# Attention over 8192 context rows on one core: turned keys made two stages early, written to device memory and read back

## What is computed

```
q = xn @ Wq                      # 128 x 1024 per batch
k, v = split(ctx @ Wkv)          # 2048 x 1024 each per batch
q = l2norm(q) * q_scale;  k = l2norm(k) * k_scale      # per head of 64
sim = einsum('bhid,bhjd->bhij', q, k) * 8
out = softmax(sim) @ v           # with the null key and value in front
return layer_norm((out, heads joined) @ Wout, g_out)
```

## Time and profile before

| | us |
|---|---|
| median of 3 runs | 1401.02 (1400.99 to 1401.05) |
| the profiled execution's own time | 1405.52 |
| its span | 1403.7 |
| PE busy in it | 1220.3 (87%) |
| DVE, ACT, POOL busy | 641.4, 439.2, 314.4 |
| the long block's loop, first query product to last output | 787.66 to 1320.96 |

### The profile page before, as it was taken

How to read it: one execution, slowest core, us unless ns; L and a number is a source line. 1 busy time by engine, 2 the same in 40 slices (tenths; PEclk the granted TensorE clock), 3 DMA queues, 4 the chain that set the end, 5 groups by cost and what they waited for, 6 DMA issues and landing times.

```text
span 1403.7 us, 12934 instructions
## 1 busy us (share of the span) xinstructions
PE 1220.3 (87%) x4726; PEld 700.7 (50%) x4726; DVE 641.4 (46%) x1098; ACT 439.2 (31%) x550; POOL 314.4 (22%) x94
## 2 busy tenths in 40 slices
PE   7999578987779998776597899999999999999558
PEld 4666233744656662453486544454445444544534
DVE  2487573134459886222522343334334333433344
ACT  2466313331346552241110523322332232233011
POOL 0000000000000000000000066655663665566000
PEclk8999799985879998797588999999999999999569
DMA  8000000030000002005000000000000000000100
GB/s 349 42 1 1 0 0 0 1 120 0 1 0 1 0 1 90 0 1 224 1 1 0 1 15 19 19 16 16 19 19 12 19 19 16 15 19 7 64 3 7
DMA packets 21365, 40.02 MB, mean 29 GB/s; under 512 B 2496, under 2 KB 18880, under 8 KB 19648
## 3 DMA queue, kind: packets, MB, share of 16 engines
q1 hardware_dynamic: 21312, 39.30, 7.7%
HBM read 39.03 MB, written 0.26 MB: 28 GB/s over the span
## 4 chain that ended last, share of the span: by engine, by line
PE 80%; DVE 11%; ACT 6%; issue 2%; POOL 1%; DMA 0%; POOLq 0%; DVEq 0%; ACTq 0%
PE PSUM L1814 15%; PE PSUM L1818 15%; PE PSUM L1389 8%; PE PSUM L1460 3%; PE PSUM L1421 3%; PE PSUM L1398 2%; PE PSUM L1451 2%; PE PSUM L1549 2%; PE PSUM L1560 2%; PE PSUM L1415 2%; PE PSUM L1843 1%; PE PSUM L1849 1%; DVE ARENA L867 1%; PE PSUM L1924 1%; PE PSUM L1745 1%
## 5 line engine op out<-in xcount | busy, mean ns | idle before, releaser
L420 POOL TENSOR_TENSOR ARENA<-ARENA 128x2048 f32<-128x2048 f32 x64 | 288.7, 4512 | 196.2 <-ACT ARENA L654 196.2
L1230 DVE TENSOR_TENSOR ARENA<-PSUM,RK 128x512 f32<-128x512 f32 x256 | 175.7, 691 | 271.6 <-PE PSUM L1814 269.3
L1814 PE MATMUL PSUM<-ARENA,CK 128*128 128x512 f32 x512 | 257.3, 606 | 5.1 <-DVE ARENA L1230 4.3
L1818 PE MATMUL PSUM<-ARENA,CK 128*128 128x512 f32 x512 | 252.8, 597 | 5.8 <-ACT ARENA L676 3.7
L654 ACT ACTIVATE ARENA<-ARENA,CK 128x2048 f32<-128x2048 f32 x64 | 128.1, 2002 | 349.7 <-DVE ARENA L1230 349.7
L1818 PEld LDWEIGHTS PSUM<-ARENA,CK 128*128 128x128 f32 x512 | 97.6, 191 | 131.7 <-issue 113.2
L1814 PEld LDWEIGHTS PSUM<-ARENA,CK 128*128 128x128 f32 x512 | 97.6, 194 | 126.2 <-issue 97.7
L363 POOL TENSOR_TENSOR RSTD<-VE,MHALF 128x4 f32<-128x4 f32 x17 | 17.2, 1009 | 614.8 <-DVE VE L721 614.8
L1389 PE MATMUL PSUM<-WK,CT 128*128 128x512 f32 x256 | 122.9, 603 | 0.0
L450 ACT ACTIVATE SQ<-PSUM 128x512 f32<-128x512 f32 x128 | 76.3, 597 | 72.4 <-PE PSUM L1389 64.6
L743 DVE TENSOR_REDUCE RK<-SQ 128x8 f32<-128x512 f32 x128 | 84.1, 681 | 14.6 <-ACT SQ L450 12.5
(11 more groups left out here) (362 smaller groups left out, 1518.1 us busy)
## 6 DMA issues: line engine op xcount, KB each, us to landing
CT<-in_ctxT SPq DMA_DIRECT2D x4, 1024.0 KB, 10.4
CK<-in_l0f_experts SPq DMA_DIRECT2D x1, 4096.0 KB, 23.5
CK<-in_ctxk SPq DMA_DIRECT2D x1, 4096.0 KB, 12.5
ARENA<-in_l2f_experts SPq DMA_DIRECT2D x2, 2048.0 KB, 8.3
CK<-in_ctxT SPq DMA_DIRECT2D x64, 64.0 KB, 1.8
CK<-in_ctxr SPq DMA_DIRECT2D x64, 64.0 KB, 1.9
ARENA<-in_l2f_experts SPq DMA_DIRECT2D x1, 3072.0 KB, 14.3
WB<-in_wb SPq DMA_DIRECT2D x1, 2738.5 KB, 11.2
```

The costliest lines, as they stand in the source:

```text
L420: nc.gpsimd.tensor_tensor(LS[b % 2], LS[b % 2], PR[:, k % 2, :], ALU.add)\
L1230: ve.tensor_tensor(PR[:, k % 2, c * 512:(c + 1) * 512].rearrange("p (j n) -> p j n", j=4), PSUM[:, c % 2, :].rearrange("p (j n) -> p j n", ...
L1814: mm(bank(c % 2), CTT[:, k, :], qpb[:, b, c * 512:(c + 1) * 512], start=True, stop=True)\
L1818: return mm(bank(4 + c), CKT[:, k, :], PR[:, k % 2, c * 512:(c + 1) * 512], start=first, stop=final, skip_group_check=True)
```

## The change

The kernel forms turned keys after all, and does it in the two early loops. There, `WK` is now the loaded operand and 512 context rows stream past it (`key_rows`): the result is two heads' keys for 512 rows, head features down the partitions. ACT copies them to one of four buffers `KEEP_T` (`keep_keys`), SP writes each buffer (256 KB) to device memory, POOL squares it into one of six buffers `KSQ` (`key_squares`), and PE sums the squares over each head's 64 partitions with a product by a selection matrix of 32 columns (`add_squares`: four products of 512 columns, to PSUM partitions 0, 32, 64 and 96). Eight times per loop the sums are copied and turned back (`turn_norms`, four transposes). DVE has no part in it any more.

In the long block, `QP` is not made. The keys are read back 2 MB at a time (four tiles), the scores are products over 64 rows, value rows are formed as `CT` tile times value weights, and the outputs add up directly in two PSUM banks, even heads in partitions 0 to 63, odd heads in 64 to 127. The null key enters by products in front of the loop, the denominators by products with ones. The two layer norms in a row before `L0_attn` and `L3_xattn` are made from one set of statistics.

```diff
-            def key_norms_pe(n0, n):
-                for m in range(n0, n0 + n):
-                    t, c = m // 2, m % 2
...
-                    mm(bank(5 + 2 * c), CT[:, t * P:(t + 1) * P], WK[:, c * 512:(c + 1) * 512],
-                        start=True, stop=True).then_inc(sem("key_rows"), PE.sends("key_rows"))
+            def key_rows(units):
+                for n in units:
+                    if n >= 2:
+                        nc.tensor.wait_ge(sem("keys_kept"), n - 1)
+                    mm(bank(5 + 2 * (n % 2)), WK[:, (n % 8) * P:(n % 8 + 1) * P], CT[:, (n // 8) * 512:(n // 8 + 1) * 512],
+                       start=True, stop=True).then_inc(sem("key_rows"), PE.sends("key_rows"))
+
+            def add_squares(halves):
+                for h in halves:
+                    nc.tensor.wait_ge(sem("key_squares"), 4 * h + 4)
...
+                    for j in range(4):
+                        last = mm(PSUM[32 * j:32 * j + 32, 0, :], w("l3x_pick")[:, 32 * (h % 2):32 * (h % 2) + 32],
+                                  KSQ[(4 * h + j) % 6], start=h % 2 == 0, stop=h % 2 == 1, skip_group_check=True)
+                    last.then_inc(sem("key_squares_added"), PE.sends("key_squares_added"))
+
+            def turn_norms(groups):
+                for g in groups:
+                    nc.tensor.wait_ge(sem("key_norms_kept"), g + 1)
+                    for j in range(4):
+                        last = tp(PSUM[:, 0, j * P:(j + 1) * P], NRM[:, j * P:(j + 1) * P], ident)
+                    last.then_inc(sem("key_norms_turned"), PE.sends("key_norms_turned"))
...
+            def key_squares(n0):
+                for n in range(n0, n0 + 64):
+                    nc.gpsimd.wait_ge(sem("keys_kept"), n + 1)
+                    if n >= 6:
+                        nc.gpsimd.wait_ge(sem("key_squares_added"), (n - 6) // 4 + 1)
+                    nc.gpsimd.tensor_tensor(KSQ[n % 6], KEEP_T[n % 4], KEEP_T[n % 4], ALU.mult)\
...
+            def keep_keys(units):
+                for n in units:
+                    nc.scalar.wait_ge(sem("key_rows"), n + 1)
+                    if n >= 4:
+                        nc.scalar.wait_ge(sem("key_squares"), n - 3)
+                        nc.scalar.wait_ge(sem("dma_keys%d" % (n % 4)), 16 * (n // 4))
...
+            def scores(t):
...
+                for half in range(2):
+                    if t:
+                        nc.tensor.wait_ge(sem("l3x_scores_taken"), 4 * (t - 1) + 2 * half + 2)
+                    for j in range(4):
+                        c = 4 * half + j
+                        for i in range(2):
+                            last = mm(PSUM[:, 2 + 2 * half + i, j * P:(j + 1) * P],
+                                      KG[DH * i:DH * (i + 1), g % 2, c, (t % 4) * P:(t % 4 + 1) * P],
+                                      QSC[DH * i:DH * (i + 1), c, b * P:(b + 1) * P], start=True, stop=True)
...
+            def values(t):
+                nc.tensor.wait_ge(sem("l3x_probs"), 2 * t + 2)
+                nc.tensor.wait_ge(sem("l3x_value_rows_kept"), 2 * t + 2)
+                for c in range(8):
+                    for i in range(2):
+                        at = ((c // 4) * 2 + i) * 512 + (c % 4) * P
+                        last = mm(PSUM[DH * i:DH * (i + 1), 6 + c // 4, (c % 4) * P:(c % 4 + 1) * P],
+                                  VT[:, t % 2, (2 * c + i) * DH:(2 * c + i + 1) * DH], PR[:, t % 2, at:at + P],
+                                  start=False, stop=t % KEY_TILES == KEY_TILES - 1, skip_group_check=True)
...
+            def finish_sums(b):
+                nc.tensor.wait_ge(sem("l3x_summed"), KEY_TILES * (b + 1))
+                take(0)
+                take(1)
...
             def finish_sums(b):
...
+                nc.vector.wait_ge(sem("l3x_l"), b + 1)
+                ve.reciprocal(L9INV[:, 0:512], bank(0))
+                ve.reciprocal(L9INV[:, 512:1024], bank(1)).then_inc(sem("l3x_l_kept"), DV.sends("l3x_l_kept"))
                 nc.vector.wait_ge(sem("l3x_l_kept"), DV.sent("l3x_l_kept"))
```

More of the change, by code:

```diff
@@ L305, in build, with key_plan, turn_of @@
         PICK2 = ARENA[0:16, 2048 + PAIRS * 3 * P:2048 + PAIRS * 3 * P + 16 * DH]
+        def key_plan(n0):
+            plan, n, added = [], n0, n0 // 4
+            for g in range(16):
+                first, second = (3, 2) if g < 8 else (2, 2) if g < 14 else (0, 0)
+                halves = list(range(added, n // 4))
+                halves = halves[:2 - added % 2]
+                turns = [h // 2 for h in (plan[-1][2] if plan else []) if h % 2]
+                plan.append((list(range(n, n + first)), list(range(n + first, n + first + second)), halves, turns))
+                added, n = added + len(halves), n + first + second
+            assert added == n // 4 and not plan[-1][2]
+            return plan
+        work_v, work_o = {}, {}
+        turns = [0]
+        def turn_of(table, at):
+            table[at] = turns[0] % 2
+            turns[0] += 1
+        turn_of(work_v, 0)
+        turn_of(work_v, 1)
+        for t in range(TILES):
+            if t > 1 and t % KEY_TILES == 1:
+                turn_of(work_o, t // KEY_TILES - 1)
+            if t + 1 < TILES:
+                turn_of(work_v, 2 * t + 2)
+                turn_of(work_v, 2 * t + 3)
+        turn_of(work_o, B - 1)
         block = ctx.enter_context(nc.Block())
@@ new lines, in _ @@
+            probs(0, 0)
+            probs(0, 1)
+            for t in range(TILES):
+                if t and t % KEY_TILES == 0:
+                    nc.scalar.wait_ge(sem("l3x_values"), t)
+                    nc.scalar.wait_ge(sem("l3x_out_kept"), t // KEY_TILES - 1)
+                    act(OT8, PSUM[:, 6:8, :].rearrange("p c n -> p (c n)"), ACT.Copy).then_inc(sem("l3x_o_kept"), AC.sends("l3x_o_kept"))
+                if t + 1 < TILES:
+                    probs(t + 1, 0)
+                    probs(t + 1, 1)
@@ new lines, in _ @@
+            for t in range(TILES):
+                more = t + 1 < TILES
+                begins = more and (t + 1) % KEY_TILES == 0
+                ends = t and t % KEY_TILES == 0
+                if more:
+                    scale(t + 1, 0)
+                    scale(t + 1, 1)
+                if t and t % KEY_TILES == 1:
+                    finish_out(t // KEY_TILES - 1) if t > 1 else None
+                if more:
+                    value_rows(t + 1, 0)
+                    scale(t + 1, 2)
+                    scale(t + 1, 3)
+                    value_rows(t + 1, 1)
+                if begins:
+                    begin_sums((t + 1) // KEY_TILES)
+                if ends:
+                    finish_sums(t // KEY_TILES - 1)
@@ L1410, in core_pe @@
                     last.then_inc(sem("probs_turned"), PE.sends("probs_turned"))
[L1411 to L1412 removed]
+                    add_squares(halves)
+                    key_rows(second)
                     nc.tensor.wait_ge(sem("pt_ready"), PE.due("pt_ready"))
@@ L1890, in _ @@
-            nc.tensor.wait_ge(sem("l3x_z_kept"), PE.due("l3x_z_kept"))
+                freed[k] = ("l3x_out_kept", b + 1)
+            scores(0)
+            for t in range(TILES):
+                more = t + 1 < TILES
+                if more:
+                    scores(t + 1)
+                if t > 1 and t % KEY_TILES == 1:
+                    finish_out(t // KEY_TILES - 1)
+                if more:
+                    value_rows(t + 1, 0)
+                    value_rows(t + 1, 1)
+                if t and t % KEY_TILES == 0:
+                    finish_sums(t // KEY_TILES - 1)
+                if t % KEY_TILES == 0:
+                    null_values(t // KEY_TILES)
+                values(t)
```

525 lines of the change are left out of this document (231 added, 294 removed).

## The result

The changed kernel takes 1362.1 us (median of four runs, 1349.08 to 1365.67) against 1401.03 (1400.99 to 1401.47): a ratio of 0.9705, 95% interval 0.9641 to 0.9768. Two further sets of runs gave 0.9651 (0.9612 to 0.9691) and 0.9661 (0.9643 to 0.9678). The profiled execution took 1361.8 us, its span is 1359.8. The forecast, 1358, is a ratio of 0.969 to the median of the kernel before. By medians the gain is 38.9 us in this set and 50.3 and 47.0 in the other two, where 43 were forecast.

The account below looks back on a forecast made before the run. PE bounds the kernel. From the profiled 1405.5 us, +77 (early loops) - 118 (long block) - 3 (norms) = 1361.5; the median runs 4.5 lower, 1357, stated as 1358. Range 1325 to 1412.

Parts of the forecast that it names:

- The tile: Long block: scores 1.79, value rows 1.72, values 1.79, division changes 0.27; 5.57 us instead of 6.87, PE still the bound.
- three changes 0.27: Long block, each tile: three changes of the array's division at 0.09 us each.
- The early loops: Each loop grows by 38.5 us: transposes 7.1, selection-matrix products 23.4, new waits 8; both by 77.
- 16 x (1.28 + 0.18): Early loops: sixteen fours of selection-matrix products, 1.28 us each plus two division changes, 23.4 us per loop.
- PE sees about six instructions ahead: Early loops' selection-matrix products: quarters one to three start at once, the fourth after the first record, so 1.28 us.
- Strict order: Rival, 10%: matmuls start and end in program order; four square products cost 2.14 us instead of 1.28, +28, 1386.
- The front: Long block before the first scores: last query's copy 1.2, 16 null products in pairs 6.9, exp 2.0; 10.3 with signals.
- A batch's end: Long block, three times: products 5.4 us plus PE waits 4.8 (2.6 for the reciprocal, 2.2 for value rows' bank).
- The tail: Last batch's end, nothing covering it: POOL's sum, reciprocal, scaling and output steps lie bare, 16 us.
- Column parts in turn: Rival, 12%: column parts run one after another in values, sums, null values and squares; +198, 1556 us.
- Instructions too dense: Rival, 12%: at 34 ns an instruction, scores and values take 2.2 us each, a tile 6.4; +51, 1409 us.
- better: Rival, 11%: quarters all at once (-13) and the early loops' waits covered (-8); 1337 us.

Follow-up runs that it names:

- values on one side: Changed kernel with odd heads' value products written to PSUM partitions 0 to 63 like even heads'; 1457.1 us, ratio 1.0386 to the kernel before.
- in one quarter: Changed kernel with all four selection-matrix products of a half group written to PSUM partitions 0 to 31; 1437.3 us, ratio 1.0219 to the kernel before.

## Why the prediction was right

**The tile** (5.57 on record, 5.80 measured, +15 us over 64). Pairs in column halves hold (shown: values on one side) and in row halves too (16 score products in 1.99 us, where one after another they would be 3.57), and PE keeps the bound, with POOL idle 1.26 us a tile. The step that was mis-sized is "three changes 0.27": they take 0.50, 0.17 on the average (an added one took 0.20). The 0.09 came from two blocks of the early loop whose division differs by rows only the earlier trace rows: there was no row of the changes that a tile really makes.

**The early loops** (+77 on record, +58.5 measured). The term that was mis-sized is "16 x (1.28 + 0.18)": the four quarters run at once. From the transposes' last record at their own pace (0.11) to the next key product it is 1.09 us and not 1.46: 12 of the 18.5 us. The step behind it that failed is "PE sees about six instructions ahead", read from the earlier trace rows: the first product in the fourth column quarter of the null scores stands behind 12 others, 48 instructions, in the kernel's order, and all first eight records of these start within 0.09 us (854.45 to 854.53). Why the second row half came 0.55 us late in rows 6 stays open. The waits were 6.2 a loop for the 8 on record, in the places named: 2.3 twice where two halves meet, 0.9 at the copy. That makes 16. Most of the rest stands behind the loops, where nothing was on record: from the last values to the next transposes it was 2.78 and 2.05 us and is 1.20 and 1.31, 2.3 less in all. Before, DVE still had a key sum to make there (L743, until 140.73 us), and only then the reciprocal and the scaling that PE waits for; after, the reciprocal is done ahead of the last values.

**Strict order** was the rule weighed, and gave 2.14 us per four. The Trainium skill, page "TensorE: Matmul & The Clock Gate", Part 3, says that matmuls start and end in program order; here three quarters' first records start ahead of the first quarter's second one (493.53 before 493.97), so that for the two records of a float32 product and those of the next product it does not hold, if they are issued product by product (in one quarter they run so). The Trainium skill gives on the same page 2.38 times for three column tiles; that agrees in kind, since four took 1.00 us here and 3.55 in one quarter.

**The front** (10.3 on record, 7.1 measured). The first scores come 26.15 us after the block's start, where the first product over 64 rows of the kernel before came after 19.0. The null scores are the reason:

```profile
854.45 1.99 PE L1884 MATMUL PSUM<-ARENA,WB 64*32 64x512 f32 x32
858.62 2.06 PE L1899 MATMUL PSUM<-ARENA 64*128 64x128 f32 x32 [2.19 <-ACT WB L698]
```

Sixteen products of 512 columns in 2.0 us: row halves times column quarters, eight at once; I had them in pairs (6.9). Of these 4.9 us, 1.2 are taken back by the last query's copy, which ends 21.6 us after the block's start instead of 20.5; the rest is not taken apart.

**A batch's end** (10.2 on record, 9.7 measured). The size was right, one half of the mechanism was not: the wait for the scaled outputs is there, 2.3 for "2.6"; the "some 2.2 more when value rows wait for their bank" is 1.8 at another place, where the sums wait for the banks. It took three experiments to see, since the profile names POOL.

**The tail** (16 on record, 18.8 measured, from the end of the last exp to the end of the last output copy):

```profile
1272.68 3.75 PE L1939 MATMUL PSUM<-CK,W 128*128 128x128 f32 x16 [8.03 <-DVE W L1307]
```

In the loop the same sixteen records take 2.02. The stages of this product at the tail and in the loop, with the granted clock behind the busy times:

```profile
1272.60:1276.40 3.80, 3.72 (x16) 3.48 (x16) 0.00 (x0) 0.00 (x0) 0.00 (x0) 0.50 0.00 0
971.80:973.60 1.80, 1.79 (x16) 1.80 (x17) 1.06 (x2) 0.70 (x1) 0.00 (x0) 1.00 0.00 0
```

0.50 against 1.00: at the tail PE had been idle for 8 us behind 2 us of work, and came back at 1.2 GHz. That I had not priced. The reciprocals' part (6.6) was as said.

Together +14.7 - 3.2 - 1.6 + 2.8 (tile, front, batch ends, tail), less the 2.1 that I had kept for signals, is +10.6; the long block came out 9.8 above the sum.

**Transfers**: hidden, as said, also when doubled. **Norms**: -3 on record. From the first statistics (DVE's `BATCH_NORM_STATS2`) to the next transposes of PE a pair took 7.64 us before (147.01 to 154.65, 759.15 to 766.79) and takes 5.96 and 5.97 after (179.83 to 185.79, 824.63 to 830.60): 3.3 less in all, as said. The stretches that hold them came out at +1.4 and -0.4 all the same; the other 4.4 us in them stand in blocks that the change does not touch, with as many products, at a lower granted clock: 232.9 us at 0.84 before and 235.9 at 0.81 after (154.65 to 387.52, 185.79 to 421.72), 229.1 at 0.80 and 230.4 at 0.79 (530.03 to 759.15, 594.24 to 824.63).

**The total.** That 1358 lies among 1357.0, 1359.5 and 1362.1 is in part luck. The mechanism held (PE is the bound, pairs in halves, hidden transfers, the places of the waits), but two terms of opposite sign were off by 18.5 and 9.8 us, and single executions differ by as much.

**Rivals.** Column parts in turn: 1556 would have been the time if it held for values, sums and squares; the two experiments that force it for values and for squares took 100 and 80 us more than the changed kernel's 1357. Instructions too dense: 32 records and 32 loads in 1.9 us are reached. Strict order fell with the squares; "better" was half right: the quarters run all at once, but the waits are not covered.

## What to carry to other kernels

Small products that fill only half or a quarter of the array are cheap as long as neighbours lie in different parts of it: two, four and eight ran at once here (float32), and writing all of them to one place cost 1.9 times for halves and 3.6 times for quarters. Count the changes of the array's division then, 0.1 to 0.2 us each, and gather products of one kind. And when a wait of an engine is put down to one that had been done for microseconds, list all semaphores of that instruction, the freeing of its target banks among them, and move one at a time.

## What had not been expected of the hardware

- Eight products of 64 rows and 32 columns at once (2 x 4 parts of the array): sixteen of 512 columns in 2.0 us.
- A change of the array's division costs 0.17 us on the average in the long block (an added one 0.20), some 0.1 in the early loops (1.00 for four quarters at once, whose product is 0.86, and 0.09 ahead of them).
- After 8 us of idleness PE ran at the lower level of its clock (3.75 us for what takes 2.02), and the granted clock ahead of the first loop differed between executions of one kernel (0.67 and 0.83 in the same ten us), which goes with most of the scatter of the profiled ones.
- Logarithm and exp of 1024 columns with two table loads, 4.7 us on ACT, are faster than DVE's reciprocal, 6.6.
